# Attention inputs as one contiguous piece per partition, the context loaded first, the residual in two halves

## The reference, cut to what matters

```python
def _L0_xattn_ref(hidden_q, kv_c, Wq, w_kc_q, w_kc_kv, W_qr, W_kr, Wo):
    q_hk = (hidden_q @ Wq.T).reshape(Bv, Sv, H, K)
    q_big = _apply_rope(einsum('bshk,hkq->bshq', q_hk, w_kc_q), ...)
    kv_r = _apply_rope(kv_c, sin_k[None], cos_k[None])
    q_r = einsum('bshq,hqr->bhsr', q_big, W_qr)
    k_r = einsum('bld,hdr->bhlr', kv_r, W_kr)
    attn = softmax(einsum('bhsr,bhlr->bhsl', q_r, k_r))
    ctx_c = einsum('bhsl,bld->bhsd', attn, kv_r)
    ...
    return ctx @ Wo.T

x = x + tanh(g_xattn[0]) * _L0_xattn_ref(_layernorm(x), ctx_512, ...)
x = x + tanh(g_ffn[0]) * _L0_ffn_ref(_layernorm(x), ...)
x = x + tanh(g_xattn[1]) * _L1_xattn_ref(_layernorm(x), ctx_512, ...)   # 16 heads, causal
x = x + tanh(g_ffn[1]) * _L1_ffn_ref(_layernorm(x), ...)                # 7 experts, top 2, one shared
```

## Time and profile before, and how to read it

| | |
|---|---|
| time, median of 3 runs (lowest to highest) | 2217.43 us (2213.9 to 2219.85) |
| time of the profiled execution | 2218.61 us |
| its span, first to last instruction | 2216.9 us |
| PE busy | 1946.2 us, 88% of the span |
| DVE, ACT, POOL busy | 64%, 43%, 23% |
| read from DRAM, written to it | 132.59 MB, 20.51 MB |
| mean granted TensorE clock | 0.942 of full speed |

### The profile page before, as it was taken

The page is one execution under the profiler, slowest core; times in us unless marked ns, Lnnn a source line. Parts: engine busy times, 40 slices in busy tenths (PEclk is TensorE's granted clock), DMA queues, the critical chain, the costliest instruction groups (busy, mean ns, idle before and its releaser), DMA issues. The chain is left out here.

```text
span 2216.9 us, 33553 instructions
## 1 busy us (share of the span) xinstructions
PE 1946.2 (88%) x11866; PEld 1541.6 (70%) x11866; DVE 1421.1 (64%) x2759; ACT 959.1 (43%) x1983; POOL 509.1 (23%) x469
## 2 busy tenths in 40 slices
PE   1899999999499999999913999799959989999997
PEld 1677787777377777877711555466639879999996
DVE  3666666676666666666767777366664544666663
ACT  1333344443233333344465333355524425666663
POOL 3211010110311110001022000133220354565553
PEclk9999999999699999999956999899985999999999
DMA  5200000000321001000051000000013147777774
GB/s 135 74 6 33 37 37 37 37 1 1 76 74 38 2 35 37 37 37 1 1 227 63 0 0 0 1 1 1 1 61 98 40 126 166 236 237 232 230 238 99
DMA packets 39530, 154.61 MB, mean 70 GB/s; under 512 B 5472, under 2 KB 12848, under 8 KB 29050
## 3 DMA queue, kind: packets, MB, share of 16 engines
q1 hardware_dynamic: 27170, 128.39, 16.5%
q0 software_dynamic: 11408, 23.37, 5.8%
q10 hardware_dynamic: 840, 1.36, 0.2%
HBM read 132.59 MB, written 20.51 MB: 69 GB/s over the span
## 5 line engine op out<-in xcount | busy, mean ns | idle before, releaser
L608 DVE TENSOR_TENSOR la_q_roped<-banks,la_rope_q 128x400 f32<-128x400 f32 x384 | 197.9, 567 | 45.6 <-PE banks L400 28.6
L555 ACT ACTIVATE la_probs<-banks,la_minus_max 100x361 f32<-100x361 f32 x256 | 145.0, 566 | 157.2 <-DVE la_minus_max L643 157.2
L643 DVE TENSOR_REDUCE la_minus_max<-banks 100x1 f32<-100x361 f32 x256 | 135.7, 530 | 58.9 <-PE banks L426 52.1
L1751 DVE TENSOR_TENSOR ex_weights_low<-ex_raw_weights,ex_weights_high 128x2048 fp32r<-128x2048 f32 x60 | 137.4, 2290 | 51.2 <-ACT ex_weights_high L1658 48.5
L343 POOL TENSOR_TENSOR la_wq_high<-la_weights,zero 128x1024 fp32r<-128x1024 f32 x14 | 26.5, 1894 | 609.6 <-PE banks L372 609.6
L435 PEld LDWEIGHTS banks<-identity,la_probs 100*121 100x121 f32 x768 | 113.4, 184 | 64.3 <-DVE la_probs L650 29.6
L446 PE MATMUL banks<-la_probs_t,la_kv_rows 121*128 121x200 f32 x768 | 151.3, 333 | 0.0
L925 PE MATMUL banks<-qf_sign_weights,qf_x_quant_t 128*100 128x512 bf16 x512 | 122.9, 391 | 32.2 <-DVE qf_hidden L1006 18.1
L573 ACT COPY la_probs_t<-banks 121x300 f32<-121x300 f32 x256 | 106.2, 415 | 96.3 <-PE banks L435 96.3
L2007 POOL TENSOR_TENSOR ex_g_low<-ex_g,ex_g_high 128x256 fp32r<-128x256 f32 (+1 forms) x104 | 86.7, 949 | 232.6 <-ACT ex_g_high L1690 232.1
L435 PE MATMUL banks<-identity,la_probs 100*121 100x100 f32 x768 | 125.6, 272 | 16.0 <-DVE la_probs L650 14.5
(11 more groups left out here) (312 smaller groups left out, 5501.6 us busy)
## 6 DMA issues: line engine op xcount, KB each, us to landing
ex_raw_weights<-w_exp SPq DMA_DIRECT2D x60, 1024.0 KB
la_weights<-w_pack SPq DMA_DIRECT2D x16, 1984.0 KB, 7.8
qf_raw_weights<-w_ffn SPq DMA_DIRECT2D x2, 4096.0 KB
qf_raw_weights<-w_ffn SPq DMA_DIRECT2D x2, 2048.0 KB
out<-ex_block_out POOLq DMA_DIRECT2D x13, 256.0 KB, 4.4
residual<-x SPq DMA_DIRECT2D x1, 3200.0 KB
normed_rows<-ex_xn SPq DMA_DIRECT2D x16, 200.0 KB
out<-residual SPq DMA_DIRECT2D x4, 800.0 KB
```

The costliest lines, as they stand in the source:

```text
L555: act.activation(prob[:, s % 4, 0:L], ps[0:S, s % 2, 0:L], ACT.Exp, bias=nmax[:, s % 4:s % 4 + 1], accum_out=sums[:, s % 4:s % 4 + 1]).the ...
L608: dve.tensor_tensor(roped[:, h, v, c, :].rearrange("p (b s) -> p b s", b=GB), ps[:, B_BANKS[k % 2], 0:NT].rearrange("p (b s) -> p b s", b=GB),
L643: dve.tensor_reduce(nmax[:, s % 4:s % 4 + 1], ps[0:S, s % 2, 0:L], AX.X, ALU.max, negate=True).then_inc(s_max, 1)
L1751: dve.tensor_tensor(wl[:, m, :], raw[:, m, :], wh[:, m, :].bitcast(F32), ALU.subtract).then_inc(w_low[m], 1)
```

## The change

The host now lays out `x` with the token first (100 by 16 by 512), the context as `ctx_rows` (half, 121 partitions, 8 batches, 3 chunks, 128), with zeros in the places behind row 361, and the latents as a tensor of their own (100 by 16 by 128). So the half context is one transfer with one run of 12,288 B per partition, and GpSimd neither zeroes the pad nor is waited for by SP. The residual goes in two transfers, with a run of 16,384 B per partition each. SP's order in half 0 is now context, residual of batches 0 to 7, first weights, residual of batches 8 to 15; the last has a semaphore of its own, `x_rest`, for which SP waits in the second block ahead of its loop. The latents are loaded with one run of 8,192 B per partition. The bytes moved stay the same but for the zero rows. ACT's transfers and all waits on `tabs` stay as they are.

```diff
--- before.py
+++ after.py
@@ -162,8 +162,8 @@
         xn = [wts[1][0:S, 4 * LCN * DC + i * D:4 * LCN * DC + (i + 1) * D] for i in range(2)]
 
         ns = NormSems(core, tag)
-        x_loaded, const_ready = sem("x_loaded"), sem("const_ready")
-        pads_zero, kv_loaded, tabs = sem("pads_zero"), sem("kv_loaded"), sem("tables_loaded")
+        x_loaded, x_rest, const_ready = sem("x_loaded"), sem("x_rest_loaded"), sem("const_ready")
+        kv_loaded, tabs = sem("kv_loaded"), sem("tables_loaded")
         ident_zero = sem("ident_zero")
         turn, kept, kv_roped = sem("turn"), sem("kept"), sem("kv_roped")
         kv_t, kv_high, kv_low = sem("kv_transposed"), sem("kv_high"), sem("kv_low")
@@ -176,15 +176,12 @@
         with nc.Block() as block:
             @block.sync
             def _(sp):
+                sp.dma_start(raw, ctx_in[half]).then_inc(kv_loaded, 16)
                 if first:
-                    sp.dma_start(core.x[:], x_in.rearrange("b s d -> s b d")).then_inc(x_loaded, 16)
-                sp.wait_ge(pads_zero, 1)
-                for c in range(LCN):
-                    n = min(LC, L - c * LC)
-                    sp.dma_start(raw[0:n, :, c, :],
-                                 ctx_in[b0:b0 + HB, c * LC:c * LC + n, :].rearrange("b p d -> p b d")
-                                 ).then_inc(kv_loaded, 16)
+                    sp.dma_start(core.x[:, 0:HB, :], x_in[:, 0:HB, :]).then_inc(x_loaded, 16)
                 sp.dma_start(w0[:], w_pack[0]).then_inc(w_in[0], 16)
+                if first:
+                    sp.dma_start(core.x[:, HB:B, :], x_in[:, HB:B, :]).then_inc(x_rest, 16)
 
             @block.scalar
             def _(act):
@@ -212,7 +209,6 @@
 
             @block.gpsimd
             def _(pool):
-                pool.memset(raw[:, :, LCN - 1, :], 0.0).then_inc(pads_zero, 1)
                 pool.memset(prob[:, :, L:LC * LCN], 0.0)
                 pool.memset(kvh[:, :, L:LE].bitcast(F32), 0.0)
                 pool.memset(kvl[:, :, L:LE].bitcast(F32), 0.0)
@@ -225,7 +221,7 @@
                                        fill=1.0, base=0, pattern=[[-1, 128]],
                                        channel_multiplier=1).then_inc(ident_zero, 1)
                 pool.wait_ge(tabs, 32 if not first else 64)
-                pool.wait_ge(kv_loaded, 16 * LCN)
+                pool.wait_ge(kv_loaded, 16)
                 half_d = DC // 2
                 for i in range(HB):
                     t = turned[:, i % 2]
@@ -252,7 +248,7 @@
                     dve.wait_ge(x_loaded, 16)
                 norm_stats_dve(dve, core, ns, tiles)
                 dve.wait_ge(tabs, 32 if not first else 64)
-                dve.wait_ge(kv_loaded, 16 * LCN)
+                dve.wait_ge(kv_loaded, 16)
                 for i, t in enumerate(tiles):
                     dve.tensor_tensor(kv[:, i], raw[:, i], trigk[:, 0], ALU.mult).then_inc(kept, 1)
                     if i >= 2:
@@ -326,6 +322,8 @@
             @block.sync
             def _(sp):
                 sp.dma_start(wts[1][:], w_pack[1]).then_inc(w_in[1], 16)
+                if first:
+                    sp.wait_ge(x_rest, 16)
                 with sp.Fori(1, PAIRS // 2) as i:
                     for par in range(2):
                         n = i * 2 + par
@@ -1077,7 +1075,7 @@
 
     def load(self, sp, w_att, ctx_in):
         sp.dma_start(self.all, w_att).then_inc(self.loaded, 16)
-        sp.dma_start(self.lat, ctx_in[:, 0:S, :].rearrange("b p d -> p b d")).then_inc(self.lat_loaded, 16)
+        sp.dma_start(self.lat, ctx_in).then_inc(self.lat_loaded, 16)
 
     def split(self, pool, zero):
         pool.wait_ge(self.loaded, 16)
@@ -2161,15 +2159,15 @@
 TILES = SH_TILES + RT
 
 
-def build(nc, x, ctx_512, g_xattn, g_ffn, w_pack, rope_q, rope_k, w_ffn, w_att,
+def build(nc, x, ctx_rows, latents, g_xattn, g_ffn, w_pack, rope_q, rope_k, w_ffn, w_att,
           w_exp, b_exp, b_down, w_router, b_router, order, tokens, out):
     with ExitStack() as ctx:
         core = Core(nc, ctx)
         for half in range(2):
-            latent_attention(core, half, x, ctx_512, g_xattn, g_ffn, w_pack, rope_q, rope_k, half == 0)
+            latent_attention(core, half, x, ctx_rows, g_xattn, g_ffn, w_pack, rope_q, rope_k, half == 0)
             core.end_stage()
         with ExitStack() as shared:
-            wa = quantised_ffn(core, w_ffn, shared, w_att, ctx_512)
+            wa = quantised_ffn(core, w_ffn, shared, w_att, latents)
             core.end_stage()
             causal_attention(core, wa)
             core.end_stage()
@@ -2187,7 +2185,12 @@
 def layouts(np, inputs):
 
     a = {k: np.asarray(v) for k, v in inputs.items()}
-    arrays = {k: np.ascontiguousarray(a[k]) for k in ("x", "ctx_512", "g_xattn", "g_ffn")}
+    arrays = {k: np.ascontiguousarray(a[k]) for k in ("g_xattn", "g_ffn")}
+    arrays["x"] = np.ascontiguousarray(a["x"].transpose(1, 0, 2))
+    c = np.zeros((B, LCN * LC, DC), np.float32)
+    c[:, :L] = a["ctx_512"]
+    arrays["ctx_rows"] = np.ascontiguousarray(c.reshape(2, HB, LCN, LC, DC).transpose(0, 3, 1, 2, 4))
+    arrays["latents"] = np.ascontiguousarray(a["ctx_512"][:, :S].transpose(1, 0, 2))
     wq = a["L0_xattn_Wq"].reshape(PAIRS, 256, KC, 128).transpose(0, 3, 2, 1).reshape(PAIRS, 128, -1)
     kc = a["L0_xattn_w_kc_q"].reshape(PAIRS, 2, DK, CQ).transpose(0, 2, 1, 3).reshape(PAIRS, 128, -1)
     wr = a["L0_xattn_W_qr"]
```

## The result

The changed kernel takes 2226.66 us (median of 7 runs, 2220.16 to 2228.98) against 2215.57 us before (7 runs beside it): ratio 1.0047, 95% interval 1.0031 to 1.0064. It is slower by 0.5%; the forecast was 12.9 us faster.

The account below looks back on a forecast made before the run. Late transfers at the start of both halves bound the kernel; gains of 10.5 us in the first and 2.4 in the second, 12.9 in all, gave 2204.5 us from a median of 2217.4, range 2192 to 2212.

Parts of the forecast that it names:

- What bounds the kernel: Start of both halves: late transfers hold the engines; first half, DVE waits 29.1 us for residual, POOL 36.9 for context.
- How the queues share: Both hardware queues with work advance by equal piece counts whatever the size; ACT's 39 per engine hold tables until 27.6 us.
- rival 1: Start of both halves: tables are not held back by large pieces; gains 14.7 and 7.3 us, 2195.4 us; chance 0.33.
- On how many engines: Start-up transfers: 100-row residual uses ten of 16 engines, 121-row context eleven; all 16 would gain some 5 us more.
- What a piece costs: Start-up transfers, priced by size from weight transfers: 0.475 us per context piece, 0.634 per residual piece; tables' pieces 0.141.
- the sum of the turns: First half: SP's pieces let through during ACT's 39 turns take 20.9 us, ACT's own 2.9; tables in at 27.6.
- Rival 2: Start of both halves: context and residual pieces keep twice the price per byte; 8.1 us slower, 2225.5 us; chance 0.05.
- The latents and the second residual half: Second residual half lands by 31 us, read at 570; latents issued at 1195.43, read at 1409.41: both cost nothing.
- The clock: After each pause matmuls start at half speed; 1.3 us either way per half, 2.6 in the range, zero in the sum.

## Why the prediction was wrong, point by point

- **What bounds the kernel** was right: both halves wait for transfers, and each microsecond taken from these waits is taken from the time.
- **How the queues share** was right, against rival 1. One piece for one piece holds with large pieces too. The Trainium skill's rule of whole packets of 9 to 17 descriptors (DMA: Bandwidth & Descriptors, Queues, rings and completion order) would have let the gates through early; the 51 against 51 of the changed kernel, and its tanh at 39 us, do not bear out that outcome.
- **On how many engines** was right for the 100 rows: 62% of 16 engines is ten, also for weight pieces that wait there. But the conclusion drawn, that only the missing six engines cost, was not: each piece on the ten is dear as well, and on sixteen busy engines a piece of 64 or 96 rows is no cheaper (1.25 and 1.15 us).
- **What a piece costs** is the step that failed. It took 0.475 and 0.634 us from weight transfers, "by size". The residual's pieces measure 1.03 with 100 rows and 0.61 with 128. In the second half 103 pieces, the context's and the weights' beside them, cost 0.848 x 128 / 103 = 1.05 each, and the context's own 0.97, twice the 0.475. With 1.03 for ten pieces, twice the context's price for eleven and 0.98 for the second residual half's seven, the sum of the turns grows by 4.0 + 5.2 + 2.4 = 11.6 us, and the tables end at 39.2 instead of 27.6; the tanh ran at 39.21. In the second half the context's 5.2 us and ACT's own pieces, 0.183 x 128 / 103 = 0.23 us each where 0.141 was taken (1.6 us for nineteen), bring the wait from the forecast 15.7 us to 22.5; it measured 22.4. The structure of the sum was sound and its price for context and residual was not.
- The price lay open: the old residual cost twice the weights' price per byte, and the text said so. It was put down to runs of 2,048 B. The length of the runs was only part of it: with long runs the residual still cost 1.6 times the weights' price per byte (1.03 us for 16,384 B against 0.614 for 15,872), and only with 128 rows are the two alike (0.61).
- **Rival 2** was the case that came: slower, by a price per byte kept near twice (2.0 times the weights' for the context, 1.6 for the residual), with its sign, context pieces above 0.7 us; 2225.5 us, measured 2226.66. It had been given 0.05, on the argument that DRAM and memory side are the same as the weights'. The memory side is not: 128 rows against 100. Its terms were off, 4.1 us too late in the first half's sum and 1.5 too little in the second half's wait (2.8 against 4.3). That its total came so near is in part luck: it is 8.1 us above a median of three runs, 2217.43, and the seven runs put the kernel before at 2215.57 and the loss at 11.1.
- **The latents and the second residual half** cost nothing, as said: the stage from the causal attention's weights on is not longer. **The clock** cost 1.0 us at the second half's beginning, within the 2.6 allowed; what the mean granted clock of whole executions adds stands below.

By the stretches, 7.0 us are accounted for; the medians say 11.1 and 11.6, with lower bounds of 6.9 and 8.9. The unprofiled executions of the changed kernel lie 1 to 9 us above its two profiled ones, and this goes with the mean granted clock of each execution. Both profiles caught it at 0.942 of full speed, where its six executions take 2220.2 to 2224.5 us; its other seven, at 0.940 or 0.941, take 2226.7 to 2229.4. In 44 executions of the groups above the kernel before takes 2215.3 to 2220.2 us at 0.941 or 0.942, where its own profile lies too (0.942), and 2207.1 to 2216.1 at 0.944 or 0.945, a clock that the changed kernel never had. By the executions at 0.942 alone the two kernels are about 4.5 us apart (medians of 2217.5 and 2222.0). Open is why the mean clock of the changed kernel is more often the lower.

## What to carry to other kernels

Look up, for each transfer, how many rows it has and not only how long its runs are: loads of 100 or 121 partitions ran at about half the rate of 128 padded ones, and the padding (up to 28% more bytes) was worth 0.9% with the tables first (1.0000 to 0.9913) and 1.2% with them on ACT's queue (1.0047 to 0.9931). A small transfer that something waits for does not belong on a second queue beside large pieces, as in these runs it pays one large piece for each of its own; put it at the head of the same queue. And where a price per byte in the trace is twice that of a neighbour, find out what the two differ in before the sum takes the better one.

## What was not expected

That 2 KB of gates, in 8 B pieces, can hold a kernel for 39 us while the DMA engines move 160 to 270 GB/s (179, 265 and 163 in the stretches shown). That weights in 128 rows, waiting on ten engines behind a 100-row transfer, run at full rate there (0.58 us), while a 64-row transfer on sixteen engines runs at half (1.25 us). And that two transfers of 96 and 4 rows are better than one of 100 by only 6 us at the landing (22.8 against 28.7, with the context cut as well), where one of 128 gains 12.
